# Where TensorE turns the rows of the next expert slot: before the hidden transposes, or between up and down

## The reference, cut to what matters

```python
h2 = rmsnorm(X, norm2_w).reshape(B * S, d)
probs = jax.nn.softmax(h2 @ router_w, axis=-1)
topw, topi = jax.lax.top_k(probs, TOP_K)
topw = jax.nn.softmax(topw, axis=-1)
shared = swiglu(h2, sh_gate, sh_up, sh_down)
gate = jnp.einsum('td,edf->etf', h2, e_gate)
up = jnp.einsum('td,edf->etf', h2, e_up)
eout = jnp.einsum('etf,efd->etd', jax.nn.silu(gate) * up, e_down)
spec = jnp.einsum('etd,te->td', eout, combine)
```

## Time and profile before

| | us |
|---|---|
| median of 3 runs | 947.49 |
| lowest and highest run | 946.36, 947.91 |
| the profiled execution | 950.77 |
| its span, first to last instruction | 949.0 |

### The profile page before, as it was taken

The page is one execution under the profiler, slowest core; times in us unless marked ns, Lnnn a source line. Parts: engine busy times, 40 slices in busy tenths (PEclk is TensorE's granted clock), DMA queues, the critical chain, the costliest instruction groups (busy, mean ns, idle before and its releaser), DMA issues. The chain is left out here.

```text
span 949.0 us, 19708 instructions
## 1 busy us (share of the span) xinstructions
PE 842.3 (89%) x7404; PEld 560.6 (59%) x7405; DVE 477.6 (50%) x1097; ACT 333.8 (35%) x563; POOL 148.5 (16%) x155
## 2 busy tenths in 40 slices
PE   5989999999988949699999877999989999999994
PEld 3346666666666838466666666455646556565552
DVE  7356655655645625266667487361133334433432
ACT  1357666666642414355555222211011111111110
POOL 4000000000001314200000022027202222222221
PEclk7579999999987979799999888799999999999998
DMA  5200000000001692256955200682312222222221
GB/s 205 77 2 2 2 2 2 3 2 2 3 2 40 119 130 83 67 68 90 106 70 66 85 0 0 250 328 102 122 46 45 45 44 40 39 44 45 45 36 20
DMA packets 68488, 58.80 MB, mean 62 GB/s; under 512 B 5504, under 2 KB 60104, under 8 KB 68432
## 3 DMA queue, kind: packets, MB, share of 16 engines
q1 hardware_dynamic: 60512, 47.60, 22.2%
q0 software_dynamic: 7152, 9.38, 5.9%
q10 hardware_dynamic: 768, 1.02, 0.3%
HBM read 35.02 MB, written 22.95 MB: 61 GB/s over the span
## 5 line engine op out<-in xcount | busy, mean ns | idle before, releaser
L1100 DVE TENSOR_REDUCE fa_m<-ps 128x2 bf16<-128x512 f32 x128 | 81.8, 685 | 35.4 <-PE ps L998 34.7
L1349 POOL DMA_INDIRECT out<-ex_Y,ex_to x39 | 60.6, 1553 | 207.7 <-DVE ex_Y L1592 204.8
L1080 ACT ACTIVATE fa_PT<-ps 128x1024 f32<-128x1024 f32 x64 | 65.6, 1024 | 67.9 <-PE ps L1016 67.9
L1417 PE MATMUL ps<-ex_WG,ex_xT 128*128 x156 | 78.5, 627 | 5.0 <-ACT ex_xT L1470 0.6
L595 ACT ACTIVATE la_PT<-ps 128x512 f32<-128x512 f32 x128 | 69.5, 594 | 33.1 <-PE ps L501 33.1
L1572 DVE TENSOR_TENSOR ex_hd<-ps,ex_sl 128x512 f32<-128x512 f32 x39 | 27.0, 692 | 101.9 <-PE ps L1417 101.9
L1430 PE MATMUL ps<-ex_WD,ex_hT 128*128 x312 | 73.8, 379 | 0.9 <-DVE ex_hT L1576 0.9
L1430 PEld LDWEIGHTS ps<-ex_WD,ex_hT 128*128 128x128 f32 x312 | 59.2, 190 | 25.3 <-issue 19.3
L1417 PE MATMUL ps<-ex_WU,ex_xT 128*128 x156 | 73.3, 592 | 0.0
L628 DVE TENSOR_REDUCE la_m<-ps 128x4 bf16<-128x512 bf16 x64 | 44.3, 692 | 47.8 <-PE ps L494 46.8
L609 DVE CAST V<-ps 96x512 bf16<-96x512 f32 x64 | 43.9, 686 | 36.8 <-PE ps L466 36.8
(11 more groups left out here) (259 smaller groups left out, 1494.4 us busy)
## 6 DMA issues: line engine op xcount, KB each, us to landing
QK<-qk_parts SPq DMA_DIRECT2D x96, 128.0 KB, 5.9
qk_parts<-pj_parts SPq DMA_DIRECT2D x16, 384.0 KB, 2.8
expert_in<-SG SPq DMA_DIRECT2D x1, 5070.0 KB, 14.8
ex_XR<-expert_in SPq DMA_DIRECT2D x39, 130.0 KB, 2.1
ex_WG<-in_e_gate SPq DMA_DIRECT2D x8, 512.0 KB, 9.8
ex_WU<-in_e_up SPq DMA_DIRECT2D x8, 512.0 KB, 9.6
ex_WD<-in_e_down SPq DMA_DIRECT2D x8, 512.0 KB, 9.7
out<-HS SPq DMA_DIRECT2D x4, 512.0 KB, 3.7
```

The costliest lines, as they stand in the source:

```text
L1080: nc.scalar.activation(PT[:, grp % 2, k:k + 2], ps[:, 2 + 2 * (hp % 2):4 + 2 * (hp % 2)].rearrange("p k (j i) -> p k j i", j=2), ACT.Exp, ...
L1100: nc.vector.reduce_max(m[:, par, h], ps[:, h % 2].rearrange("p (f j) -> p f j", f=2), AX.X).then_inc(s_max, 1)
L1349: nc.gpsimd.indirect_dma_start(out=outs, out_offset=bass.IndirectOffsetOnAxis(ap=to[:, n:n + 1], axis=0), in_=Y[:, n], in_offset=None, com ...
L1417: last = mm(ps[:, bk + n], xT[:, n, cc], w[:, bass.ds(e + cc * F, F)], start=cc == 0, stop=cc == 1)
```

## The change

TensorE turns the rows of slot s+2 after gate and up of slot s+1 and before down of slot s. Slot 1 is turned ahead of the loop. Since the last trip has no slot 39 to turn, the loop runs 18 trips and the last trip is written out behind it. The other engines' programs stay as they are.

```diff
                 e = expert_of(0)
                 turn_x(0, (0, 16, False))
                 gate_up(0, 0, e)
-                with pe.Fori(0, NS // 2) as t:
+                turn_x(1, (1, 16, True))
+
+                def trip(t, more):
                     es = [expert_of(2 * t + i) for i in range(3)]
-                    turn_x(2 * t + 1, (1, t * 16 + 16, True))
                     turn_hidden(2 * t, 0)
                     gate_up(2 * t + 1, 1, es[1])
+                    turn_x(2 * t + 2, (0, t * 16 + 32, True))
                     down_slot(2 * t, 0, es[0])
-                    turn_x(2 * t + 2, (0, t * 16 + 32, True))
                     turn_hidden(2 * t + 1, 1)
                     gate_up(2 * t + 2, 0, es[2])
+                    if more:
+                        turn_x(2 * t + 3, (1, t * 16 + 32, True))
                     down_slot(2 * t + 1, 1, es[1])
+
+                with pe.Fori(0, NS // 2 - 1) as t:
+                    trip(t, True)
+                trip(NS // 2 - 1, False)
                 turn_hidden(NS - 1, 0)
                 down_slot(NS - 1, 0, expert_of(NS - 1))
```

## The result

The changed kernel takes **934.25 us** (median of 4 runs, 932.13 to 938.45), against 947.7 us for the kernel before in the same session (4 runs, 946.36 to 949.35). The ratio is 0.9859, with a 95% interval from 0.9836 to 0.9882. The forecast was 933.5 us, in a range from 931.3 to 937.8. The profiled execution took 935.86 us, its span 934.1 us.

The account below looks back on a forecast made before the run. TensorE's own sequence plus its standing still before each gate was taken to bound the kernel; 37 periods of 5.82 us instead of 6.20, plus 0.09, save 14.0 us off 947.49, giving 933.5 us, range 931.3 to 937.8.

Parts of the forecast that it names:

- The period: Slot loop on TensorE: start-to-start times sum to 5.83 us, taken as 5.82, against 6.20 before, 0.38 us a slot less.
- What the gate had waited for: Before each gate: 0.28 us waiting for ACT's copy of turned x, plus 0.09 us for an unhidden weight load.
- The weight load: Gate's first weight load: hidden behind the transposes once x is ready early, so its 0.09 us a slot goes.
- the first rival: Gate's weight load stays unhidden: the 0.28 us wait goes, 0.09 us stays, 5.92 us a slot, 937.1 us; chance 0.10.
- The two unknown prices: Turn into down, 0 to 0.06 us a slot, and trip boundary, 0 to 0.1 us for each of 18; both taken as 0.
- The trip's boundary: Branch and three expert-number loads now before the hidden transposes: taken as 0, bounded at up to 1.8 us.
- The spare times: Slack in the new order: DVE's product 1 us, DVE's hidden copy before down 1.9 us, POOL's adds 1.5 us.

Follow-up runs that it names:

- the loop's shape alone: Kernel before with its order of turns kept and only the last trip written out (18 looped trips): 948.42 us against 947.5, ratio 1.0012.
- the early start: Changed kernel with slots 0 and 1 turned and slot 0's gate and up run before waiting for the shared expert's last sum: 929.94 us, ratio 0.9825.
- those last two kernels: Two later-session kernels: x turned inside down with ACT's copy twice as wide, 966.95 us against 971.93; and the filled start, 951.17 us against 971.93.
- the filled start: Changed kernel with x of slots 0 and 1 turned around the last shared down, both gates before the first hidden tile's wait: 951.17 us against 971.93, ratio 0.9801.
- the other of the pair: Kernel turning x inside down before its last block, with ACT's copy of x made twice as wide: 966.95 us against 971.93, ratio 0.9936.
- the cover counted out: Changed order with x turned inside down, before the last of its four blocks: 932.67 us against 947.5, ratio 0.9831.

## Why the prediction was right

- **The period.** The sum took 5.82 us a slot; measured 5.82 in all five profiles of this order, at its plain copy, a wide one or another start. Hidden transposes to gate 0.44, gate to up 1.72, up to the turn 1.72, turn into down 0.21, down to hidden transposes 1.73: each term came out within 0.01 us. From the gate of slot 1 to that of slot 38, 215.3 us were forecast and 215.34 measured.
- **What the gate had waited for.** Shown from both sides: 0.44 us less cover cost 0.44 us (6.63 a slot), 0.64 us more copy cost 0.64 us (6.84), 0.16 us too little cover cost 0.16 us (5.98), and enough cover cost nothing.
- **The weight load.** The load of the gate does slip under a 128-column transpose when its data is ready: the 5.92 us a slot of the first rival was not seen. The rule of the Trainium skill ("TensorE: Matmul & The Clock Gate", Part 3), by which it would need another row group, does not hold for these loads; the load at 790.07 starts 0.11 us before the gate at 790.18, and the gate is not late.
- **The two unknown prices.** The turn between up and down, bounded at 0 to 0.06 us, costs 0 (turn to down 0.21). The trip's boundary costs 0: with the order of before and the new shape 6.20 us a slot, and in the changed kernel two neighbouring slots at 5.82 us (790.18, then 796.00 by the hidden transposes' start at 795.56 plus 0.44).
- **The spare times.** DVE's product ends at 794.51, 1.05 us before the hidden transposes (1 forecast). DVE's copy of the hidden rows ends at 792.11, 1.7 us before down (1.9 forecast). The forecast tied this copy to the hidden transposes (2.15 us from their start to its end), but in both kernels DVE comes to it from Y and the payload, and it starts 1.68 us behind the end of the down before (784.58 to 786.26, and 789.74 to 791.42). Without the turn of x between them, it ends 2.37 us behind the transposes' start. The spare time covered the slip. The load for slot 2 was issued at 697.03, its turn came at 700.50, 3.5 us later (3.5 forecast from the same two points). On POOL 1.5 us were forecast from one landing of 3.50 us. In the profile after, the landing took 3.96 us and the shortest distance of two adds is 4.82 us (919.13 to 923.95), so 1.0 us is spare. That term was sized on a single row and is the least certain of them.
- **The size that was most off is the scatter.** The range took about 1 us for it, from three runs within 1.6 us. In the two sessions where its median stayed at 947.5, runs of before went on to spread from 942.32 to 953.27 us, and the changed kernel's first four from 932.13 to 938.45, one of them outside the range. The scatter is not in the slots, which take 209.52 us for 36 periods in both profiles of the changed kernel. It lies ahead of them: with the same code there, the last shared down starts between 675.75 and 684.51 us in ten profiles. That the median of four such runs came within 0.8 us of 933.5 is in part luck, and so is the profiled span (934.1 against 935.0 forecast), where an earlier start of 1.81 us met a tail 0.84 us longer. The working of the range also has a slip: 1.1 us and 1.1 us below 933.5 are 931.3, not 931.5, and the 1.8 us allowed for the boundary is missing from the upper end, 935.7. Neither mattered.

## What to carry to other kernels

When an engine looks saturated, sum the starts of its instructions over one period and compare like with like: four transposes that take 0.72 us where two take 0.22, and two equal groups of matmuls 0.09 us apart, held a gain of 1.4% that neither the busy share nor the waits view named. Put the producer of an operand that goes through another engine so far ahead that other work covers the whole round trip (0.93 us here from the turn to the weight load, and 0.11 more for the load to hide). Once that is covered, more distance buys nothing.

A stretch that the same kernel does without the wait, such as a first trip, is a free control: here it gave the 1.72 us from gate to up and showed that the wait goes. With the starts of other rows (0.22 us for two transposes), that gave the new period to a hundredth of a microsecond before anything was run.

## What the runs showed of the hardware

The short wait of 0.55 us before slot 0's gate left the granted clock at 1.00, while the same wait behind another of 2.17 us came with a mean of 0.72 and a gate of 3.52 instead of 1.98 us. So the idle time between two stages cost 2.4 us by itself and 1.5 us more in clock. The second part varies between executions: with the same two waits, gate and up of slot 0 together take from 4.96 us (the kernel before, 692.46 to 697.42) to 5.23 us (the loop's shape alone, 688.97 to 694.20), against 3.53 us in the early start.

In the session of those last two kernels something happened that I had not expected, ahead of the slots and in both kernels profiled there. In the shared expert, TensorE stands for 16 us behind the up matmuls that start at 652.24, and DVE for 26.5 us beside it (in the kernel with the filled start; in the other of the pair TensorE's gap is 16.7 us, at the same place):

```profile
652.24 1.88 PE L1372 MATMUL ps<-V,SU 128*128 128x512 f32 x4
670.10 3.78 PE L1372 MATMUL ps<-V,SG 128*128 128x512 f32 x4 [15.98 <-issue]
```

In the other sessions this stretch is dense: from 640 to 675 us TensorE is busy throughout at 1.00 in, for example, the kernel before and the loop's shape alone. It is not tied to the chip by its number: the four runs from the loop's shape to the cover counted out have the same number on record, and the kernel before took 947.5 us beside them. The waits view names "issue" for TensorE in one kernel and DVE's product in the other, and nothing in the core's own work for DVE. No run here was made to find the cause; it is left open. The last shared down starts at 706.76 us there, 26.4 us later than in the changed kernel run again. That is close to the 24 us by which the kernel before was longer in that session, but the kernel before was not profiled in it. The ratios are taken against runs of the kernel before on the same chip in the same session.
